# Two layers of gated cross-attention: the feed-forward of layer 0 spread over twice as many steps, with the groups around it interleaved

## The reference, cut to what matters

```python
x (8,128,512)          # 8 batches of 128 tokens
for layer in (0, 1):
    # 32 query heads in 8 groups of 4, each group with one K/V head of width 128
    q = rmsnorm(layernorm(x) @ Wq.T); k = rmsnorm(ctx @ Wk.T); v = ctx @ Wv.T
    x = x + tanh(g_xattn[layer]) * (softmax(q k^T / sqrt(128) + mask) v) @ Wo.T
    if layer == 0:     # block-quantised gated FFN, hidden width 1376, blocks of 32
        h = fp6(layernorm(x)); a = silu(h @ fp4(Wg).T) * (h @ fp4(Wu).T)
        x = x + tanh(g_ffn[0]) * (fp6(a) @ fp4(Wd).T)
    else:              # 512x512 int4 weight, dequantised and permuted, plus bias
        x = x + tanh(g_ffn[1]) * (layernorm(x) @ W4[perm].T + bias)
```

## Time and profile before

| | us |
|---|---|
| median of 3 runs (lowest, highest) | 1437.88 (1436.12, 1438.23) |
| the profiled execution, its own time | 1436.61 |
| its span | 1434.8 |
| PE busy | 1364.0 (95%) |
| DVE busy | 959.0 (67%) |
| ACT busy | 846.6 (59%) |
| POOL busy | 629.4 (44%) |

### The profile page before, as it was taken

One profiled execution on the slowest core, in us unless ns is written; L12 is line 12 of the kernel. 1 busy time (PEld: TensorE's weight loads), 2 busy tenths in 40 slices (PEclk: granted clock), 3 DMA queues, 4 the chain that ended last, 5 costly groups with the idle time before them and its releaser, 6 DMA issues.

```text
span 1434.8 us, 26304 instructions
## 1 busy us (share of the span) xinstructions
PE 1364.0 (95%) x7915; PEld 1143.1 (80%) x7924; DVE 959.0 (67%) x1971; ACT 846.6 (59%) x3270; POOL 629.4 (44%) x667
## 2 busy tenths in 40 slices
PE   5999999999999999987878899999999999999897
PEld 4888888888888888864645688888888888888786
DVE  4678787887878786477777655555555555557565
ACT  4656666666666666655455566566656666665341
POOL 2437666565656575443333334333333334341132
PEclk9899999999999999998989999999999999999999
DMA  7011210211111111001000110101010100100001
GB/s 272 1 51 47 64 51 18 78 36 55 51 62 51 57 51 57 31 1 45 1 29 1 35 48 30 45 29 44 29 44 29 44 29 23 50 0 1 0 16 45
DMA packets 33688, 59.23 MB, mean 41 GB/s; under 512 B 2784, under 2 KB 25952, under 8 KB 29536
## 3 DMA queue, kind: packets, MB, share of 16 engines
q1 hardware_dynamic: 33632, 58.54, 12.3%
HBM read 56.43 MB, written 2.10 MB: 41 GB/s over the span
## 4 chain that ended last, share of the span: by engine, by line
PE 69%; issue 12%; DVE 8%; POOL 6%; ACT 3%; DMA 1%; SPq 0%; POOLq 0%; DVEq 0%; ACTq 0%
PE bank L958 49%; PE bank L950 7%; PE bank L1034 6%; PE bank L1095 5%; POOL w_lo L398 2%; DVE amax L734 1%; DVE f_q L741 1%; POOL rstd L430 1%; DVE f_s L758 1%; POOL ln_rstd L420 1%; PE bank L1086 1%; PE bank L967 1%; DVE f_iq L752 1%; ACT L534 1%; POOL x_sb L498 1%
## 5 line engine op out<-in xcount | busy, mean ns | idle before, releaser
L398 POOL TENSOR_TENSOR w_lo<-w_raw,w_hi (+1 forms) x150 | 232.5, 1563 | 208.4 <-ACT w_hi L550 207.7
L567 ACT ACTIVATE squares<-bank 128x128 bf16<-128x128 f32 x512 | 134.8, 278 | 265.4 <-PE bank L958 265.4
L855 DVE SCALAR_TENSOR_TENSOR probs<-bank,mask_sb 128x512 f32<-128x512 f32 x128 | 88.2, 689 | 228.9 <-PE bank L1034 228.8
L607 ACT ACTIVATE probs<-probs,negmax 128x128 f32<-128x128 f32 x512 | 198.6, 390 | 4.4 <-DVE negmax L859 4.0
L426 POOL TENSOR_TENSOR meansq<-sumsq,scalars 128x5 f32<-128x5 f32 x128 | 27.9, 218 | 324.7 <-ACT squares L567 324.7
L430 POOL TENSOR_TENSOR rstd<-meansq,scalars 128x5 f32<-128x5 f32 x128 | 154.1, 1204 | 10.9 <-POOL meansq L426 1.3
L808 DVE TENSOR_TENSOR oT_lo<-bank,oT_hi 128x512 fp32r<-128x512 f32 x128 | 88.2, 689 | 96.7 <-ACT oT_hi L542 96.6
L958 PE MATMUL bank<-w_hi,oT_hi 128*128 (+1 forms) x512 | 150.1, 415 | 0.0
L958 PE MATMUL bank<-w_hi,xT_hi 128*128 (+1 forms) x512 | 142.6, 401 | 0.6 <-DVE w_lo L682 0.6
L958 PE MATMUL bank<-w_lo,oT_hi 128*128 (+1 forms) x512 | 138.2, 391 | 0.0
L958 PE MATMUL bank<-w_lo,xT_hi 128*128 (+1 forms) x512 | 138.1, 392 | 0.0
(11 more groups left out here) (132 smaller groups left out, 3056.1 us busy)
## 6 DMA issues: line engine op xcount, KB each, us to landing
w_raw<-in_wq SPq DMA_DIRECT2D x16, 1024.0 KB, 4.9
w_raw<-in_wo SPq DMA_DIRECT2D x16, 1024.0 KB, 4.8
fw_raw<-in_ffn_w SPq DMA_DIRECT2D x36, 192.0 KB, 2.3
w_raw<-in_wk SPq DMA_DIRECT2D x16, 256.0 KB, 5.3
w_raw<-in_wv SPq DMA_DIRECT2D x16, 256.0 KB, 5.4
x_sb<-in_x SPq DMA_DIRECT2D x4, 512.0 KB, 9.9
ctx_raw<-in_ctxT SPq DMA_DIRECT2D x4, 512.0 KB, 10.5
out<-x_sb SPq DMA_DIRECT2D x8, 256.0 KB, 2.0
```

Source lines behind the costliest of these rows:

```text
L398: last = nc.gpsimd.tensor_tensor(lo, raw, hi.bitcast(FP32), ALU.subtract)
L567: last = nc.scalar.activation(squares[:, h // 2, (b + 1) % 4, h % 2, :], psQ[:, h * P:(h + 1) * P], ACT.Square, scale=SCALE, accum_out=sum ...
L607: last = nc.scalar.activation(probs[:, h * P:(h + 1) * P], probs[:, h * P:(h + 1) * P], ACT.Exp, bias=negmax[:, h:h + 1], accum_out=rowsum ...
L855: nc.vector.scalar_tensor_tensor(heads(probs[:, :]), heads(psSQ[:, :]), SCALE, mask_sb[:, :].unsqueeze(1).to_broadcast([P, REP, P]), ALU.m ...
```

## The change

The zone becomes 32 steps (48 to 79), and its units are no longer in plain order. With A, B the last two groups of layer 0 and C, E the first two of layer 1, the order of `zone_order` is A0-A3; B0 A4 B1 A5 B2 A6 B3 A7; B4-B7 C0-C3; E0 C4 E1 C5 E2 C6 E3 C7; E4-E7. The number of units is the same. The QUANT loop has one turn less (its last group is written out, steps 48 to 55) and so has the PLAIN loop.

For batch i the FFN now has five steps: 56+2i normalises and quantises the input ("norm"), 57+2i does the input transposes, `gate_up(0)` and `gate_up(1)` ("gate"), 58+2i does `gate_up(2)`, the remaining transposes and the down product ("down"), 59+2i adds it to x ("acc"), 60+2i makes the next layer's transposes ("next", in psA now and not psC). So odd steps hold gate of batch i and acc of i-1, even steps norm of i+1, down of i and next of i-1.

Inside a step: on PE `gate_up(2)` stands between the K/V and the Q product of the even step, and the down product is last in it; `gate_up(1)` stands after the output product, and hidden chunk 0 is transposed last in the odd step. On ACT silu(0) and silu(1) stand in the odd step on both sides of the exponentials and silu(2) in the even step ahead of the weight split. On DVE `hidden(0)` is now ahead of pT_lo, `hidden(2)` ahead of v_lo; the input is quantised at the end of the norm step. On POOL the scalings come first in the step. Weight pieces are split in steps 49 to 53 (B), 61 to 65 (C, two a step), 66 to 69 (E: 3, 3, 2, 2), and 77 to 79 (the next group, two a step, and its Wo at the end of 79). The int4 weight is unpacked in steps 75 to 78 and permuted in steps 78 and 79.

The diff, cut to its core:

```diff
-ZONE0, ZONE1 = UNITS - BATCHES, UNITS + BATCHES
+ZONE0, ZONE1 = UNITS - 2 * BATCHES, UNITS + 2 * BATCHES
...
-def ffn_tiles(s):
-    return tile(s - 60), tile(s - 61), tile(s - 62), tile(s - 63)
+def zone_order():
+    a, b, c, d = (UNITS // BATCHES + k for k in (-2, -1, 0, 1))
+    order = [(a, i) for i in range(4)]
+    for i in range(4):
+        order += [(b, i), (a, i + 4)]
+    order += [(b, i) for i in range(4, 8)] + [(c, i) for i in range(4)]
+    for i in range(4):
+        order += [(d, i), (c, i + 4)]
+    return order + [(d, i) for i in range(4, 8)]
...
+SPLIT_ZONE = {1: ((B, 0), (B, 1)), 2: ((B, 2), (B, 3)), 3: ((B, 4), (B, 5)), 4: ((B, 6), (B, 7)), 5: ((B, 8), (B, 9)),
+              13: ((C, 0), (C, 1)), 14: ((C, 2), (C, 3)), 15: ((C, 4), (C, 5)), 16: ((C, 6), (C, 7)),
+              17: ((C, 8), (C, 9)), 18: ((E, 0), (E, 1), (E, 2)), 19: ((E, 3), (E, 4), (E, 5)),
+              20: ((E, 6), (E, 7)), 21: ((E, 8), (E, 9)),
+              29: ((E + 1, 0), (E + 1, 1)), 30: ((E + 1, 2), (E + 1, 3)), 31: ((E + 1, 4), (E + 1, 5))}
+FFN0 = ZONE0 + 8
...
+            i = (s - FFN0 - first) // 2
+            return i if kind == ZONE and (s - FFN0 - first) % 2 == 0 and 0 <= i < BATCHES else None
+        self.norm, self.gate, self.down, self.acc, self.next = (tile(first) for first in range(5))
...
# POOL, step
+                if t.gate is not None:
+                    scale_six("in", t.gate)
+                if t.down is not None:
+                    scale_six(1, t.down)
+                if t.active:
                     pool.wait_ge(rinv_done, n - 1)      # probs * rinv
...
+                if t.down is not None:
+                    scale_six(2, t.down)
+                if t.acc is not None:
+                    ln_rstd_of(NORM["next", t.acc])
...
+                split_lower(split_pieces(n, b, kind, j))
+                if t.norm is not None:
+                    ln_rstd_of(NORM["ffn", t.norm])
                 if has(n, 0):
                     unit_rstd(n)
...
# ACT, step
+                if t.down is not None:
+                    silu(2, t.down)
+                    split_upper(split_pieces(n, b, kind, j))
+                if t.gate is not None:
+                    act.wait_ge(fxT_ps, t.gate + 1)     # f_xqT, ahead of the squares
...
-                    act.wait_ge(i0_ps, i_gate + 1)
-                    silu(2, i_gate)
...
# DVE, step
+                if t.gate is not None:
+                    hidden(0, t.gate)
                 if has(n, 2):
                     dve.wait_ge(pt_hid, n - 1)          # pT_lo
...
# PE, step
                     three_products(psKV[:, 0:2 * P], ...)
+                if t.down is not None:
+                    gate_up(2, t.down)
                     three_products(psQ[:, :], ...)
...
+                if t.next is not None:
+                    pe.wait_ge(ln_xn, NORM["next", t.next] + 1)
+                    pe.wait_ge(silu_done, len(CHUNKS) * min(t.next + 2, BATCHES))
+                    transposes(qn, psA, ident[:, :]).then_inc(xT_ps, 1)
...
                         three_products(psY[:, :], ...)
+                if t.gate is not None:
+                    gate_up(1, t.gate)
...
+                if t.down is not None:                  # after P V
+                    pe.wait_ge(ib_sb, t.down + 1)
...
-                if kind == LAST and n in (LAST0 + 3, LAST0 + 4):
+                for k in gathered(n, kind):             # steps 78 and 79
```

More of the change, by code:

```diff
@@ new lines, with __init__, tile @@
+SPLIT_ZONE_LATE = {31: ((E + 1, 6), (E + 1, 7), (E + 1, 8), (E + 1, 9))}
+FFN0 = ZONE0 + 8
+class Tiles:
+    def __init__(self, s, kind):
+        def tile(first):
+            i = (s - FFN0 - first) // 2
+            return i if kind == ZONE and (s - FFN0 - first) % 2 == 0 and 0 <= i < BATCHES else None
+        self.norm, self.gate, self.down, self.acc, self.next = (tile(first) for first in range(5))
+        self.active = any(i is not None for i in (self.norm, self.gate, self.down, self.acc, self.next))
+        self.last = s - LAST0 - 4 if kind == LAST and 0 <= s - LAST0 - 4 < BATCHES else None
+        self.first = s + 1 if kind == FIRST and s + 1 < BATCHES else None
@@ L77, in final_tile @@
 def final_tile(s):
-    i = s - 124
+    i = s - LAST0 - 4
     return i if 0 <= i < BATCHES else None
-def upto(i):
-    return min(max(i + 1, 0), BATCHES)
+INT4_0 = ZONE0 + 27
 def sequences():
-    norms, quants = [("x", b) for b in range(BATCHES)], []
+    norms = [("x", b) for b in range(BATCHES)]
     for s in range(ZONE0, ZONE1):
[L91 to L100, removed]
+        t = Tiles(s, ZONE)
+        if t.norm is not None:
+            norms.append(("ffn", t.norm))
+        if t.acc is not None:
+            norms.append(("next", t.acc))
@@ L162, in flamingo_kernel @@
         fw_out = sb("fw_out", [P, FW_MAX], BF16, under)
+        under.close()
+        under = ExitStack()
+        onehots = [sb(f"onehot{t}", [P, 2, D], FP32R, under) for t in range(2)]
         under.close()
@@ L550, in step @@
                     nc.scalar.activation(hi, raw, ACT.Copy).then_inc(split_hi, 1)
+            def step(n, b, kind, j, q=None):
+                t = Tiles(n, kind)
+                if has(n, 3):
+                    act.wait_ge(pv_ps, n - 2)
+                    wait(act, y_ps, n - 3)
+                    nc.scalar.activation(oT_hi[:, :], psPO[:, :], ACT.Copy).then_inc(o_hid, 1)
+                if t.down is None:
+                    split_upper(split_pieces(n, b, kind, j))
                 if has(n, 0):
@@ L860, in step @@
                                             negate=True).then_inc(nm_done, 1)
+                if t.norm is not None:
+                    if t.down is not None:
+                        dve.wait_ge(clipped, SIX[2, t.down] + 1)
+                    normalise(NORM["ffn", t.norm], t.norm, f_s[:, :])
                 if has(n, 0):
@@ new lines, in step @@
+                for k in gathered(n, kind):
+                    pe.wait_ge(w4_done, 5)
+                    pe.wait_ge(xT_lod, 2 * BATCHES)
+                    wait(pe, wp_hid, k)
+                    wait(pe, wp_lod, k)
+                    for ps, w in ((psA, w4_hi), (psB, w4_lo)):
+                        for r in range(2):
+                            for c in range(2):
+                                last = nc.tensor.matmul(ps[:, :], onehots[r][:, c, k * P:(k + 1) * P], w[:, r, c, :],
+                                                        start=(r == 0 and c == 0), stop=(r == 1 and c == 1))
+                    last.then_inc(wp_ps, 1)
```

471 lines of the change are left out of this document (222 added, 249 removed).

## The result

The changed kernel takes 1416.04 us (median of 4 runs, 1414.92 to 1417.42), against 1437.0 us for the kernel before in the same series; the ratio is 0.9853, 95% interval 0.9837 to 0.987. In a later series it took 1416.02 us (ratio 0.9854, 0.9839 to 0.9869). The forecast was 1410, with 1391 to 1430 as its range.

A forecast was written before the change was run, and what follows sets the result against it. PE was taken to bound plain steps, with 7.0 us a batch lost to waits and lower clock around the FFN. FFN -25.0, permutation -2.6, loops 0: 1436.61 - 27.6 = 1409.0, 1410 as median; range 1391 to 1430.

The forecast's parts named there:

- The bound: PE's work fills plain steps; around the FFN 15.1 us a batch, 8.1 of it PE's work and 7.0 lost.
- The wait of 3.57 us for L758: PE idle ahead of gate_up(1) until DVE frees psA and psB; forecast to go, leaving under 0.5 us.
- The floor of 27.2 us a pair: PE's work in an odd and an even step, 19.1 + 8.1 us, if no wait were left; 34.2 before.
- the FFN's steps: Sixteen odd and even steps plus 0.4 us: 96.1 us over plain ones against 121.1, so -25.0 us.
- the permutation: int4 weight permutation, moved to steps 78 and 79: 11.4 us instead of 14.0, so -2.6 us.
- A pair without pieces: Odd step 14.2 us and even step 15.9 us, without weight splits.
- the odd step's loss: P V waits for pT_lo, behind hidden(0) on DVE: 0.8 us over PE work of 13.4, step 14.2.
- In the even step the loss: 0.4 us at the probabilities, 0.7 at hidden(2) and its scaling, 1.1 at kn, qn and pT_lo: 2.2, step 15.9.
- The weight splits: Pieces on POOL ahead of unit_rstd: rstd 1.3 us later, even steps 17.2 with two, 18.6 with three.
- I take it as full: PE's granted clock in the FFN steps: no drop expected, longest idle stretches 1 to 2 us, 3.3 in step 66.
- rival (b): Idle stretches lower PE's clock (1426 us) or table loads come onto PE's path (1430 us); chance 0.18.
- (a): FFN steps near PE's floor, 1 us lost per pair, 28.2 us a pair: 1387 us; chance 0.17.

The follow-up runs named there:

- the kernel without table loads: Copy in place of Silu in layer 0's FFN (leaves out the silu), against the changed kernel: 1399.62 us, ratio 0.976 to the kernel before.
- The experiments with pT_lo and kT: Changed kernel, odd steps: pT_lo ahead of hidden(0) on DVE, 1415.92 us; kT ahead of silu(1) on ACT, 1416.27 us; both, 1417.53 us.
- POOL's order alone: Changed kernel with unit_rstd ahead of the weight split on POOL in even steps: 1402.13 us, ratio 0.9774 to the kernel before.

## Why the prediction was right, and where its steps were off

*The bound* held: the 7 us lost per batch were waits and the lower clock behind them, and PE's own work did not change (1363.1 against 1364.0 us busy). The wait of 3.57 us for L758 is gone, as forecast, and a batch costs 12.8 us over plain steps (102.1 / 8) where it cost 15.1. The floor of 27.2 us a pair was reached by no kernel; the lowest is 28.28, without table loads. In total the changed kernel was 6 us slower than forecast: the FFN's steps gave 19.0 us instead of 25.0, the permutation nothing instead of 2.6.

*A pair without pieces* was forecast at 14.2 + 15.9 = 30.1 us and takes 30.11. The split between its steps was wrong: odd steps take 15.25 and even ones 14.86. The term that failed is the odd step's loss, put at 0.8. Against the kernel without table loads, by the starts of PE's groups in step 59, P V begins 0.8 us later for pT_lo (0.55 of it recorded as idle), as forecast, but the next K/V product comes 0.6 us late (0.46 idle) for kT, which ACT copies out of psKV only after the table load and silu(1), and I had not priced that wait. In the even step the loss was put too high: of the 1.1 us ahead of the k and q transposes and P V 0.07 is recorded as idle in step 60. The sum came out right because the chain was right from end to end: silu(1), hidden(1), hidden(2), the scaling, the moments, rstd and kn were forecast to end at 26.0 us after the start of the odd step, and kn ends at 26.1 (steps 59 and 60). The experiments with pT_lo and kT show that this ring fixes the pair, and what one step loses the other does not. That it closes on itself the forecast did not say; it went through it once, from the odd step to the even one.

*The weight splits* are the term that was mis-sized: "such a step is 17.2", and 18.6 with three pieces. They take 18.3 and 19.57. The place was right (POOL's order alone gives all of it back). Two pieces make kn 1.8 us later, not 1.3, and "I take it as full", of the clock, was false for these four steps; this is the larger part of what such a step missed, about 1.7 us each. Idle times under 2 us were enough in three of them; I had taken the 3.57 us of the earlier trace rows as the only measure of how long it may be. The rows before held another: the window of step 123 has a granted clock of 0.82, and the waits in it are one of 1.89 us and one of 0.94. In the other steps the clock stayed up. So the clock half of rival (b) was true in four steps of nineteen. The sum of the sixteen steps is 254.2 us against the 248.5 forecast: 7.3 us from the odd steps, -1.6 from the even.

*The permutation* was to give 2.6 us and gave nothing by the windows: 14.9 before, 14.3 and 0.5 after. The costs in steps 75 to 79 are 14.3 us instead of 11.4: DVE's overrun from its work of step 75, priced at nothing because of the slack behind it, makes step 76 1.9 us longer (PE waits 1.69 us for the probabilities); and in step 78 PE waits 1.17 us for them (steps 78 and 79 take 12.4 us over plain ones, at a clock of 1.00), behind DVE's unpacking, which took longer there. DVE's and POOL's timeline in step 78 of the changed kernel:

```profile
881.65 3.52 POOL L469 TENSOR_TENSOR w_lo<-w_raw,w_hi 128x512 fp32r<-128x512 f32 x2 [3.87 <-ACT w_hi L612]
882.37 1.66 DVE L856 CAST w_hi<-w 128x1024 fp32r<-128x1024 f32 x1
...
884.62 1.10 DVE L895 TENSOR_TENSOR probs<-probs,rinv 128x512 f32<-128x512 f32 x1
```

The cast took 0.69 us for the first part of the weight (at 863.33), the scaling of the probabilities takes 0.68 there (at 864.60), and POOL was idle as each of them began; POOL's two pieces take 3.52 us instead of the 2.68 of the earlier trace rows. The Trainium skill, "SBUF — State Buffer", section "Who interferes with whom", says that VectorE operations with two SBUF inputs, or in a two-port mode, and GpSimd's share a pair of ports that one of them holds for its whole instruction. The longer durations on both engines agree with it; no run took one of them away, so that this is the cause was not tried.

*The rivals.* (a), near the floor, with 28.2 us a pair, is what the kernel without table loads comes to (28.28). Rival (c) had its place right, POOL's unit_rstd behind other work, but at 1.9 to 3.1 us in four steps and not 3.7 in sixteen. Rival (b)'s table loads: three of them are on the ring, and taking all out gives 1.8 us a pair, since PE, then busy for 28.08 of 28.28 us, comes next.

## What to carry to other kernels

When an FFN or the like is spread over several steps of a pipeline, follow the dependencies round until they meet themselves in the next period: the length of that ring is the period, as long as it is over PE's own work. Moving an instruction that stays on the ring, or was never on it, changes only which wait carries it; what helps is to take one off the ring, as the splits here (15.1 us) and, where no split ran, the normalisation (0.7 us a step). Ahead of a small operation that two engines and PE wait for (here POOL's rstd) put nothing that can come after it; that one order was worth 14 us here, two thirds of what the change itself gave. An idle time of PE can cost more than its length where dense bf16 matmuls follow it.

## What was not expected of the hardware

Idle times of PE of 1.9 us, in steps with transposes and fp32 products around them, were followed by the lower clock in most places: 3.56 us for eleven matmuls that take 2.2 to 2.4. In two of 18 such steps, with 1.90 and 1.91 us idle, they were not. Eight unused matmuls in that idle time kept it up and made the kernel 5.3 us faster. DVE's operations lengthen in places where POOL is busy (the normalisation 0.54 and 1.14 us, above); no run took POOL's work away alone, so its part in that stays an inference.
